# FC2 of a Swin block: the 64-channel rest in two row tiles of 64, and the scaled result in SBUF

## The reference

```
f   = roll(layernorm(x, g1, b1), (-3, -3))
win = window_partition(f)                      # 64 windows of 49 tokens per image
q, k, v = split(win @ w_qkv + b_qkv)           # 96 -> 3 * 96
a   = softmax(q k^T * 8**-0.5 + mask)          # per window and head
f   = x + roll(window_reverse((a v) @ w_proj + b_proj), (3, 3))
h   = gelu(layernorm(f, g2, b2) @ w_fc1 + b_fc1)     # FC1: 96 -> 192
out = f + h @ w_fc2 + b_fc2                          # FC2: 192 -> 96
```

## Time and profile before

| | |
|---|---|
| time, median of 3 runs (lowest to highest) | 2865.55 us (2864.36 to 2867.81) |
| span of the profiled execution | 2865.7 us |
| PE busy (matmuls) | 2765.1 us, 96% |
| PEld busy (weight loads) | 2312.9 us, 81% |
| DVE busy | 2349.2 us, 82% |
| ACT busy | 2136.4 us, 75% |
| POOL busy | 1810.7 us, 63% |
| mean granted clock of TensorE | 0.991 of full |
| a pair of steps | 21.7 us: `contract` loads its first weights at 501.67 us in one even step and at 1411.93 us 42 pairs later |
| share of the last chain by engine | PE 91%, ACT 4%, issue 2%, DVE 2%, POOL 1% |

### The profile page before, as it was taken

One profiled execution on the slowest core, in us unless ns is written; L12 is line 12 of the kernel. 1 busy time (PEld: TensorE's weight loads), 2 busy tenths in 40 slices (PEclk: granted clock), 3 DMA queues, 4 the chain that ended last, 5 costly groups with the idle time before them and its releaser, 6 DMA issues.

```text
span 2865.7 us, 137800 instructions
## 1 busy us (share of the span) xinstructions
PE 2765.1 (96%) x55491; PEld 2312.9 (81%) x55491; DVE 2349.2 (82%) x6634; ACT 2136.4 (75%) x3464; POOL 1810.7 (63%) x2344
## 2 busy tenths in 40 slices
PE   4899999999999999999999999999999999999997
PEld 2788888888888888888888888888888888888885
DVE  7788888888888888888888888888888888888885
ACT  2677777777777777777777777777777777777774
POOL 3566666656666666666665665666666666666565
PEclk7999999999999999999999999999999999999998
DMA  2544545444554544454455455454455445454441
GB/s 72 135 125 129 132 124 132 128 130 127 131 133 125 132 131 126 129 132 124 127 132 131 125 133 133 125 132 131 126 132 132 124 129 129 129 132 128 131 117 35
DMA packets 414850, 358.86 MB, mean 125 GB/s; under 512 B 63646, under 2 KB 414176, under 8 KB 414204
## 3 DMA queue, kind: packets, MB, share of 16 engines
q1 hardware_dynamic: 414220, 350.04, 46.8%
HBM read 193.29 MB, written 154.14 MB: 121 GB/s over the span
## 4 chain that ended last, share of the span: by engine, by line
PE 91%; ACT 4%; issue 2%; DVE 2%; POOL 1%; SPq 0%; DMA 0%; POOLq 0%; DVEq 0%
PE psum L529 19%; PE psum L511 11%; PE psum L652 9%; PE psum L437 9%; PE psum L493 8%; PE psum L569 7%; PE psum L554 6%; PE psum L617 6%; PE psum L447 6%; ACT probs L713 4%; PE psum L607 3%; PE psum L455 3%; PE psum L472 2%; PE psum L596 1%; DVE nmax L849 0%
## 5 line engine op out<-in xcount | busy, mean ns | idle before, releaser
L713 ACT ACTIVATE probs<-psum 113x784 f32<-113x784 f32 x768 | 633.2, 824 | 358.9 <-PE psum L511 341.4
L849 DVE TENSOR_REDUCE nmax<-psum 113x16 f32<-113x784 f32 x768 | 745.1, 970 | 97.1 <-PE psum L493 97.0
L529 PE MATMUL psum<-vbd,probs 128*49 128x18 f32 x24576 | 642.4, 197 | 7.6 <-issue 7.0
L398 POOL TENSOR_SCALAR ve<-mv 112x7 f32<-112x7 f32 (+1 forms) x264 | 65.9, 250 | 915.0 <-PE psum L569 672.8
L529 PEld LDWEIGHTS psum<-vbd,probs 128*49 128x49 f32 x24576 | 632.2, 126 | 10.7 <-issue 10.5
L511 PE MATMUL psum<-qbd,kst 128*49 128x196 f16 x6144 | 404.7, 250 | 34.4 <-DVE xfl L884 5.7
L493 PE MATMUL psum<-kbd,qst 128*49 128x196 f16 x6144 | 404.5, 250 | 5.3 <-DVE nmax L849 3.4
L405 POOL TENSOR_TENSOR rs<-ve,half 112x7 f32<-112x7 f32 (+1 forms) x264 | 394.7, 1495 | 0.0
L410 POOL TENSOR_TENSOR xn<-xn,rs 112x672 f32<-112x672 f32 (+1 forms) x264 | 342.6, 1298 | 73.9 <-POOL rs L405 73.9
L884 DVE TENSOR_TENSOR xfl<-psum,xfh 96x784 f16<-96x784 f32 (+1 forms) x264 | 252.9, 958 | 160.7 <-ACT xfh L725 159.6
L873 DVE BATCH_NORM_STATS2 st<-tok 112x6 f32<-112x96 f32 x1824 | 318.1, 246 | 59.0 <-ACT tok L720 45.0
(11 more groups left out here) (96 smaller groups left out, 6129.4 us busy)
## 6 DMA issues: line engine op xcount, KB each, us to landing
stack_pages<-nat SPq DMA_DIRECT2D x256, 294.0 KB, 3.0
kst<-stack_pages SPq DMA_DIRECT2D x256, 220.5 KB
qbd<-stack_pages SPq DMA_DIRECT2D x1024, 55.1 KB
stack_pages<-nat SPq DMA_DIRECT2D x256, 147.0 KB, 2.0
xr<-in_x_dram SPq DMA_DIRECT2D x224, 147.0 KB, 2.7
out_dram<-yr SPq DMA_DIRECT2D x224, 147.0 KB, 2.3
qst<-stack_pages SPq DMA_DIRECT2D x256, 73.5 KB
kbd<-stack_pages SPq DMA_DIRECT2D x1024, 18.4 KB
```

The source lines that it names most:

```text
L529: last = nc.tensor.matmul(dst[:, :, h, :], probs[:, b.c % 2, h // 4, p, h % 4 * L:(h % 4 + 1) * L], vbd[:, b.c % 4, p * NH + h, :, :], sta ...
L713: nc.scalar.activation(probs[0:PR, b.c % 2, u, :, :].rearrange("j (g q) k -> j g (q k)", g=2), wide_bank()[0:PR, LEFT:LEFT + 8 * SPAN].rea ...
L849: nc.vector.tensor_reduce(dst, psum[0:PR, A:A + 2, 0:2 * CH].rearrange("i g (q h j) -> i g q h j", q=2, j=L), axis=AX.X, op=ALU.max, negat ...
```

## The change

The FC2 of both bands becomes one stage, `contract(t)`. Bank D+s now holds half s of the tokens of both bands, band n in columns 196n to 196n+195. First come the three matmuls with block 0 for each band and half (12 in all, 128 rows). Then come the matmuls of the rest: each uses only the 64 rows that hold something, rows 0 to 63 of weights and data for half 0 into bank D, rows 64 to 127 for half 1 into bank D+1, alternating (12 in all). `fc2_made` is raised once, by two, after the last. ACT's `scaled` reads band n out of both banks and writes it to a new SBUF tile `ys`, and waits for `y_made` of the band two before; `result` reads `ys`; `turn` and the end of the kernel's `contract` wait for `y_scaled` where they waited for `y_made`.

```diff
+        ys = sb("ys", [C, 2, TOK])
...
-                        pe.wait_ge(y_made, t.step(STORE[1]).count(1, 1))
+                        pe.wait_ge(y_scaled, t.step(STORE[1]).count(1, 1))
...
+                for n, b in made:
+                    pe.wait_ge(hid_low, b.count(1, 1))
...
+                    for s in range(2):
                         for m, (w, h) in enumerate(((w2h, hidh), (w2h, hidl), (w2l, hidh))):
-                            last = nc.tensor.matmul(dst, w[:, weights, :], h[:, b.c % 2, part, :], start=k + m == 0, stop=k == 1 and m == 2)
-                last.then_inc(fc2_made, 1)
+                            nc.tensor.matmul(psum[0:C, D + s, n * PART:(n + 1) * PART], w[:, 0, :], h[:, b.c % 2, s, :],
+                                             start=n == made[0][0] and m == 0, stop=False, skip_group_check=True)
+                for n, b in made:
+                    for m, (w, h) in enumerate(((w2h, hidh), (w2h, hidl), (w2l, hidh))):
+                        for s in range(2):
+                            rows = slice(REST * s, REST * (s + 1))
+                            last = nc.tensor.matmul(psum[0:C, D + s, n * PART:(n + 1) * PART], w[rows, 1 + s, :], h[rows, b.c % 2, 2, :],
+                                                    start=False, stop=m == 2, skip_group_check=True)
+                last.then_inc(fc2_made, len(made))
...
-                nc.scalar.activation(psum[0:C, D + n, 0:TOK], psum[0:C, D + n, 0:TOK], ACT.Identity, bias=vec[:, BF:BF + 1], scale=1 / GAIN).then_inc(y_scaled, 1)
+                wait(act, y_made, b.count(1, -1))
+                nc.scalar.activation(ys[:, n, :].rearrange("c (s t) -> c s t", s=2), psum[0:C, D:D + 2, n * PART:(n + 1) * PART], ACT.Identity, bias=vec[:, BF:BF + 1], scale=1 / GAIN).then_inc(y_scaled, 1)
...
-                dst, src, res, inner = yr[:, b.c % 2, :, :], psum[0:C, D + n, 0:TOK], xf[:, b.c % 8, 1, :], BANDS - 1
+                dst, src, res, inner = yr[:, b.c % 2, :, :], ys[:, n, :], xf[:, b.c % 8, 1, :], BANDS - 1
```

More of the change, by code:

```diff
@@ L634, in expand_rest, with contract @@
                     rest((B, A)[n], w1h, w1l, b, 1).then_inc(fc1_made, 1)
-            def contract(t, n):
-                b = t.step(RESULT[n])
-                if not has(b):
+            def contract(t):
+                made = [(n, t.step(RESULT[n])) for n in range(2) if has(t.step(RESULT[n]))]
+                if not made:
                     return
[L640 to L650, removed]
-                        for m, (w, h) in enumerate(((w2h, hidh), (w2h, hidl), (w2l, hidh))):
-                            last = nc.tensor.matmul(dst, w[:, weights, :], h[:, b.c % 2, part, :], start=k + m == 0, stop=k == 1 and m == 2)
-                last.then_inc(fc2_made, 1)
+                for n, b in made:
+                    pe.wait_ge(hid_low, b.count(1, 1))
+                    if n == made[0][0]:
+                        if turns(t.step(TURN)):
+                            pe.wait_ge(tokens_in, t.step(TURN).count(1, 1))
+                        else:
+                            wait(pe, y_scaled, b.count(1))
+                    if first(b, 0):
+                        pe.wait_ge(w2_wide, 2)
+                    for s in range(2):
+                        for m, (w, h) in enumerate(((w2h, hidh), (w2h, hidl), (w2l, hidh))):
+                            nc.tensor.matmul(psum[0:C, D + s, n * PART:(n + 1) * PART], w[:, 0, :], h[:, b.c % 2, s, :],
[7 more added lines that the diff above has]
+                last.then_inc(fc2_made, len(made))
@@ L691, in step @@
                     project(t)
-                    contract(t, 0)
-                    contract(t, 1)
+                    contract(t)
             steps(pe, step)
```

## The result

The changed kernel takes 2876.58 us (median; 2871.29 to 2881.17) against 2867.81 us (2864.36 to 2869.22) for the kernel before on the same chip: a ratio of 1.0031 with a 95% interval of 1.0020 to 1.0042. So it is slower by some 9 us, 6 to 12 by the interval, in the place of no difference. Its profiled execution has a span of 2879.4 us.

A forecast was written before the change was run, and what follows sets the result against it. The prediction took `n_low`, not FC2, to hold the odd step's start. It summed 2865.7 us + 0 (FC2) + 0 (`scaled`) + 0 (`turn`) + 0 to 6 (`result`) to 2866 us, range 2815 to 2925.

The forecast's parts named there:

- What bounds the kernel: Start of the odd step on PE: it waits for `n_low` from DVE, and FC2 ends some 0.18 us too early to matter.
- No change: Whole kernel: the time stays the same, by itself 2861 to 2872 us; chance 0.58.
- the contention of the copies: Second `result` against POOL's copies and L410, beyond the slack: 0.05 to 0.75 us a pair, 2872 to 2962 us; chance 0.14.
- The matmuls: FC2 on PE: six pairs of row tiles at 0.09 us; 1.64 us in place of 2.02, 0.38 us shorter.
- the rival that they don't: FC2's row tiles don't overlap: FC2 0.09 us longer, time still 2866 us; counted within the likeliest case, no separate chance.
- The gain of 47 us: FC2's saving reaching the time, predicted as 128 x 0.38 = 49 us, to 2817 us; full gain 0.05, part 0.08.
- One signal for both bands: ACT's `scaled` of the first band starts only after all FC2 matmuls; the later start is covered by slack, cost 0.
- `result` reads SBUF twice: DVE's second `result` beside POOL: some 0.45 us late, slack just covers it; 0 to 0.05 us a pair, upper bound 96 us.
- `turn`, cost 0: `turn` on PE no longer waits for `result`; it did not wait before, so nothing is won.
- The power instruction holds DVE: First `result` waits for POOL's L405, making PE 1.1 us late a pair: 141 us, 3007 us; chance 0.15.
- The sum: Whole kernel: 2865.7 us plus 0 for FC2, `scaled` and `turn`, plus 0 to 6 for `result`, so 2866 us.

The follow-up runs named there:

- e9: The kernel before with FC2's 24 matmuls kept but the 12 of the rest cut to 3 columns; 2865.16 us against 2864.62, ratio 1.0002.
- e5: The kernel before with `n_low` made earlier: ACT does `back_high` ahead of `queries_keys_high`, DVE `back_low` ahead of `residual`; 2827.58 us, ratio 0.9867.
- e10: The changed kernel with `n_low` made early and the odd step's second `result` moved behind `by_token`; 2797.65 us, ratio 0.9771.
- e11: The same schedule as e10 with the old FC2 of 24 matmuls and a signal for each band, result still in SBUF; 2830.98 us, ratio 0.9886.
- e8: The kernel before with only the joint signal: `fc2_made` raised by two after the second band's matmuls; 2870.0 us, ratio 1.0010.
- e2: The changed kernel with the scaled result left in PSUM, `result` in four parts and waiting for both bands' `scaled`; 2872.07 us, ratio 1.0020.
- e1: The kernel before with only the scaled result written to SBUF, read there by `result`, and its waits; 2872.85 us, ratio 1.0022.
- e12: The changed kernel with only the odd step's second `result` moved behind `by_token`; 2881.64 us, ratio 1.0052.
- e3: The kernel before without the 12 matmuls of FC2's rest, so channels 128 to 191 are missing; 2904.2 us, ratio 1.0129.
- e4: The kernel before with the first half of the tokens multiplied twice in FC2, 12 matmuls more a pair, same output; 2958.93 us, ratio 1.0319.

## Why the prediction was right and where it was off

*What bounds the kernel.* Right, and shown from four sides: the load of L512 still stands 0.22 us behind the end of L891; the wait ahead of it grew by 0.37 us a pair; e9 is shorter in FC2 and no quicker; and with `n_low` early e5 begins the step 0.17 us behind FC2.

*The forecast.* "No change" was put at 2861 to 2872 us by itself, and 2876.6 lies outside that: there is a change, small and clear of noise. The range held it because it was made wide for the contention of the copies.

*The matmuls.* 1.57 us from first to last start, for which the terms give 1.64 less the last pair's 0.09, 1.55; so 0.37 us saved for 0.38. The row tiles do overlap, and the rival that they don't is refuted. The gain of 47 us was there, and none of it shows in the pair; e10 against e11 shows it arriving.

*One signal for both bands, cost 0.* Off. It holds in the repeating pair (e8: 21.56), and `scaled` took 0.58 us from PSUM into SBUF as in place (0.55). But I sized it by that pair alone. When the pipeline empties nothing covers the first band's wait for the second: 3.6 to 4.3 us by the profiles of the changed kernel and e2, and 3.5 (0.3 to 5) by the time of e8, which has the signal alone. The other row-tiled kernels end in 42.3 to 44.7 us, so the size is known to some 2 us only.

*`result` reads SBUF twice, 0 to 6 us, taken as 0.* The mechanism was right and the size taken was at the wrong end. The second `result` is 0.49 us longer (estimated 0.45) and POOL's first copy 0.28. The second `maxima` begins at +3.44 us of the step in place of +3.22, and its slack covers all but 0.03 us. The dozen or so pairs with POOL late, which I did not look for, account for most of the 4 us by which the excess of pairs without a stall grows. e1 measures 6.3 us for the whole of it.

*`turn`, cost 0.* Right by the profiles: the loads of `turn` wait 48.8 us in all in the changed kernel and 49.1 before. That it no longer needs the second `result` became worth something only in e10.

*The power instruction holds DVE.* Refuted: the first `result` took 0.69 us inside L406. The Trainium skill (SBUF — State Buffer, Who interferes with whom) has a DVE instruction with two SBUF inputs wait for the end of a GpSimd instruction that reads SBUF. By the profile that fits L411 and the copies (1.17 us in place of 0.68), and not an instruction on seven columns a row (0.69 inside its 1.51).

*The sum.* By the profiles the changed kernel is 13.7 us longer in span (its profiled run is the slowest of its seven, so this is more than the 8.8 us between the medians): 0.03 x 128 = 4 for the undisturbed pairs, 4 for the other long ones, 3 for more stalls in `weighted`, 4 for the end, less 1 for an earlier first pair (134.2 us against 135.4). By the times, e1 and e8 add up to 6.3 + 3.5 = 9.8 us, and e1 and e2, which split the change the other way, to 6.3 + 5.5 = 11.8; 8.8 were measured. Since the stalls differ by several us from kernel to kernel, 5.0 between e12 and the kernel before, neither sum is a proof of each share.

## What to carry to other kernels

A stage's share of the last chain is no bound on what it costs: look for the event that the next stage waits for, and measure the distance to it with and without the stage. A saving that is swallowed by a wait is still there; move the work that the wait hangs on (here two lines in two queues, 39 us) before or along with it. And size a removed overlap also where the pipeline fills and empties, not in the repeating pair alone.

## What the runs showed of the hardware

**PE stalls in the middle of a stream, at places that move evenly.** `weighted` issues 96 matmuls of 18 columns at some 0.026 us each, the densest stretch of the kernel. All loads of one stage are one line of code with no wait among them, and yet PE stops there for 0.2 to 1 us. Timeline of PEld in the kernel before, four of these places (the number behind the x is how many loads follow the stop):

```profile
225.57 0.76 PEld L529 LDWEIGHTS psum<-vbd,probs 128*49 128x49 f32 x29 [0.45 <-issue]
...
269.27 0.67 PEld L529 LDWEIGHTS psum<-vbd,probs 128*49 128x49 f32 x26 [0.41 <-issue]
...
356.76 0.58 PEld L529 LDWEIGHTS psum<-vbd,probs 128*49 128x49 f32 x21 [1.02 <-issue]
...
530.36 0.30 PEld L529 LDWEIGHTS psum<-vbd,probs 128*49 128x49 f32 x9 [0.57 <-issue]
```

They lie two pairs (43.7 us) or about a multiple of that apart, and each time three or four matmuls later in the stage: x29, x26, (none at 313), x21, then x9 and on to x2. Stalls at the same load numbers come back in all kernels that have 24 FC2 matmuls a pair, e9 among them. The DMA part of the page for e3, for the kernel before and for e4 (packets, MB, share):

```profile
q8 instruction: 435, 7.13, 1.0%
```

```profile
q8 instruction: 447, 7.32, 1.1%
```

```profile
q8 instruction: 459, 7.52, 1.1%
```

12 matmuls a pair more or fewer, each with its load, are 3072 instructions in 128 pairs, and they are 12 packets: one packet, of 16.4 KB, for 256 instructions. 447 in 128 pairs are 3.5 a pair, so that the border between two packets comes back to nearly the same instruction every second pair; with 435 it is 3.4, the borders are spread over the step, and e3's stalls come 110 us, five pairs or 17 packets, apart and at many places (44 pairs with one). The Trainium skill (Runtime: NRT & Kernel Launch, Instruction fetch mechanics) states refills in blocks of 16 KiB or 256 instructions, and calls the cost of crossing one mostly hidden; the sizes agree, and "mostly" here leaves 11 us in the kernel before.

That the stalls are PE waiting for its next packet is borne out by counting in the traces. In the kernel before, from one stall of the repeating pairs to the next there are always a whole number of packets and 124.1 loads for each (869 loads and 7 packets, or more). The load behind the stop begins 2.3 to 3.0 us after a packet of this queue starts, in all 18; only 7% of L529's loads lie there. No run moved the packets by themselves.

The same count shows what decides whether a border costs anything: how long before its load is due the packet starts. Taken are the loads of `weighted` at the numbers at which the stalls lie, in the 12 kernels with 24 FC2 matmuls, wherever the last packet had started 1.0 to 3.6 us before the load was due:

| packet started before the load was due by | loads | of these with a stall |
|---|---|---|
| under 2.2 us | 97 | 97 |
| 2.2 to 2.7 us | 196 | 64 |
| over 2.7 us | 166 | 1 |

The median of this lead is 2.40 us in the kernel before, 2.24 in e12 and 2.91 in e5, and 18 of 32, 22 of 41 and 2 of 36 such loads stall. Open is what starts a packet sooner or later. It isn't just PE's idle time ahead of the odd step: beyond the 0.17 us that the change of tiling takes, that is 0.64 us in e9, which has less excess from stalls than the kernel before with its 0.19 (8.5 against 10.8 us), and 0 in e10, which still has 8.3. The kernels with few stalls also repeat best: e5's runs lie within 1.2 us, e12's within 11.

**Row tiles.** Two matmuls of 64 rows and 96 columns of weights side by side, 196 columns each, start 0.08 to 0.09 us after the pair before (0.12 behind the first), as one matmul of 128 rows does; going from full rows to row tiles costs 0.09 to 0.10 us, and going on to the column tiles of L512 0.09 (e10).
